# Attention stage: two moves of the softmax sums issued by SyncE one half pair later, the tanh ahead of the copy of the sums

## The reference

```python
xn = _layernorm(x, axis=-1)
# attention on xn
q = (x @ Wq.T + bq).reshape(B, S, N_HEADS, D_K)
...
scores = jnp.einsum('bqhd,bkhd->bhqk', q, k) * SCALE
mask = _local_mask(S)[None, None]          # (j <= i) & (j >= i - 128)
scores = jnp.where(mask, scores, jnp.float32(-10000.0))
attn = jax.nn.softmax(scores, axis=-1) + jnp.float32(1e-09)
ctx = jnp.einsum('bhqk,bkhd->bqhd', attn, v).reshape(B, S, D_MODEL)
return ctx @ Wo.T + bo
...
# feed forward on xn: 2 of 8 experts by gate, and one shared expert
h = jax.nn.silu(g) * u
eo = jnp.einsum('bem,emh->beh', h, down_proj_w)
combined = jnp.einsum('beh,be->bh', eo, c)
...
x = x + attention + combined + shared_out
```

## Time and profile before

| | |
|---|---|
| median of 3 runs | 1829.69 us (1823.14 to 1830.5) |
| profiled execution | 1809.16 us, its span 1807.4 us |
| TensorE busy | 1631.9 us (90%) |
| VectorE, ScalarE, GpSimd busy | 1157.8, 967.5, 1049.6 us (64%, 54%, 58%) |
| one masked maximum (L1526), mean | 385 ns |
| one copy of sums (L1431) | 0.60 us, 64 of them |

### The profile page before, as it was taken

The page is one execution under the profiler, slowest core; times in us unless marked ns, Lnnn a source line. Parts: engine busy times, 40 slices in busy tenths (PEclk is TensorE's granted clock), DMA queues, the critical chain, the costliest instruction groups (busy, mean ns, idle before and its releaser), DMA issues.

```text
span 1807.4 us, 38460 instructions
## 1 busy us (share of the span) xinstructions
PE 1631.9 (90%) x11441; PEld 1330.0 (74%) x11441; DVE 1157.8 (64%) x3852; ACT 967.5 (54%) x1914; POOL 1049.6 (58%) x1139
## 2 busy tenths in 40 slices
PE   5888874999999999999999789989898898889987
PEld 4666663888898888888888556666676666666665
DVE  5899973666666566666656656665666666666652
ACT  3545432545545454454544356666666666666663
POOL 0888886222122221212220269888898888888888
PEclk9989996999999999999999589999999999999999
DMA  4577646444444444444564466766666666667652
GB/s 132 199 246 246 234 188 221 156 142 155 144 153 148 147 156 145 151 150 151 149 142 105 107 144 155 160 165 157 149 154 149 147 156 153 153 160 161 155 127 80
DMA packets 224801, 284.26 MB, mean 157 GB/s; under 512 B 59369, under 2 KB 143978, under 8 KB 224746
## 3 DMA queue, kind: packets, MB, share of 16 engines
q1 hardware_dynamic: 163898, 199.17, 39.4%
q10 hardware_dynamic: 47216, 47.20, 8.7%
q0 software_dynamic: 13632, 37.24, 8.3%
HBM read 193.61 MB, written 79.95 MB: 151 GB/s over the span
## 4 chain that ended last, share of the span: by engine, by line
PE 72%; POOL 9%; ACT 5%; DVE 5%; issue 4%; ACTq 3%; DMA 1%; DVEq 0%; POOLq 0%; SPq 0%
PE psum L151 42%; PE psum L817 12%; PE psum L1303 6%; PE psum L1263 5%; POOL plain_arena L389 3%; PE psum L1286 2%; POOL plain_arena L388 2%; PE psum L898 2%; ACT plain_arena L1417 2%; ACTq L1436 1%; ACTq L1437 1%; ACT plain_arena L1431 1%; DVE plain_arena L1541 1%; DVE plain_arena L1526 1%; ACT plain_arena L1449 1%
## 5 line engine op out<-in xcount | busy, mean ns | idle before, releaser
L151 PE MATMUL psum<-split_arena 128*128 128x512 f32 (+2 forms) x4560 | 1010.2, 373 | 59.4 <-DVE plain_arena L1541 55.2
L151 PEld LDWEIGHTS psum<-split_arena 128*128 128x128 f32 x4560 | 783.5, 198 | 208.0 <-DVE plain_arena L1541 57.5
L1526 DVE CUSTOM_DVE_ANT_0 plain_arena<-psum,mask 128x256 f32<-128x256 f32 (+1 forms) x1024 | 338.1, 385 | 211.7 <-PE psum L1263 211.3
L881 POOL DMA_INDIRECT plain_arena<-xn_d,order x156 | 156.5, 1003 | 509.7 <-PE psum L898 466.1
L1417 ACT ACTIVATE plain_arena<-psum 128x512 f32<-128x512 f32 (+1 forms) x512 | 250.3, 541 | 239.5 <-PE psum L1286 220.1
L817 PE MATMUL psum<-split_arena 128*128 128x256 f32 x1872 | 233.8, 285 | 0.0
L817 PEld LDWEIGHTS psum<-split_arena 128*128 128x128 f32 x1872 | 226.9, 192 | 0.1
L944 ACT ACTIVATE plain_arena<-psum 128x512 f32<-128x512 f32 x156 | 93.3, 598 | 221.1 <-PE psum L151 220.9
L995 DVE TENSOR_TENSOR plain_arena<-psum,plain_arena 128x512 f32<-128x512 f32 x156 | 107.7, 690 | 115.8 <-ACT plain_arena L944 112.8
L1263 PE MATMUL psum<-split_arena 48*128 48x256 f32 (+1 forms) x1024 | 156.7, 351 | 12.1 <-POOL plain_arena L1249 6.8
L1185 POOL TENSOR_SCALAR_AFFINE_SELECT plain_arena<-plain_arena 128x1024 f32<-128x1024 f32 x128 | 140.4, 1097 | 35.5 <-ACT plain_arena L1417 34.9
(11 more groups left out here) (163 smaller groups left out, 1869.0 us busy)
## 6 DMA issues: line engine op xcount, KB each, us to landing
plain_arena<-in_gate_w SPq DMA_DIRECT2D x39, 512.0 KB, 3.3
plain_arena<-in_up_w SPq DMA_DIRECT2D x39, 512.0 KB
plain_arena<-in_down_w SPq DMA_DIRECT2D x39, 512.0 KB, 3.5
y_d<-plain_arena ACTq DMA_DIRECT2D x39, 512.0 KB, 2.9
plain_arena<-in_x SPq DMA_DIRECT2D x32, 512.0 KB, 4.8
q_d<-split_arena SPq DMA_DIRECT2D x32, 512.0 KB, 3.6
k_d<-split_arena SPq DMA_DIRECT2D x32, 512.0 KB, 4.7
split_arena<-q_d SPq DMA_DIRECT2D x128, 128.0 KB, 3.6
```

What stands on the lines that cost most here:

```text
L151: last = pe.matmul(out, lhs_t(p), rhs(q), start=(begins and c == 0 and k == 0), stop=(ends and c == len(chunks) - 1 and k == 2), skip_grou ...
L881: pool.indirect_dma_start(c_x[:, a, :], None, xn_d, bass.IndirectOffsetOnAxis(order[:, T * blk + a:T * blk + a + 1], 0)).then_inc(c_ldx, 16)
L1526: last = dve.tensor_tensor_reduce(b_junk[:, 2 * par + i % 2, 0:cols], psum[:, par, at:at + cols], mask[:, 2 * P - cols:2 * P], -1.0, 3e38, ...
```

## The change

The two moves leave ScalarE's `copy_sums` and become `move_sums` on SyncE, one half pair later, behind what SyncE issues in the half pair before. Every later step of this route comes one half pair later as well (lags 17, 18, 19, 21, 22 and 23 become 18, 19, 20, 22, 23 and 24). In ScalarE's half pair the tanh stands ahead of the copy of the sums. Nothing is computed otherwise.

```diff
--- before.py
+++ after.py
@@ -1093,7 +1093,7 @@
 
 
         LAG_TM, LAG_M, LAG_T, LAG_SEL, LAG_V, LAG_U = 5, 6, 8, 10, 14, 15
-        LAG_RC, LAG_RS, LAG_SP, LAG_N, LAG_CH, LAG_CL = 17, 18, 19, 21, 22, 23
+        LAG_RC, LAG_RS, LAG_SP, LAG_N, LAG_CH, LAG_CL = 18, 19, 20, 22, 23, 24
 
         def turns(eng, turn):
 
@@ -1142,6 +1142,14 @@
                 sp.dma_start(b_vd[:, s, :, :], v_d[ds(b, 1), :, :, g * 64:(g + 1) * 64].rearrange(
                     "o p a c -> p (o a) c")).then_inc(b_ldv[s], 16)
 
+            def move_sums(b, g):
+                c, at = g // 2, 32 * (g % 2)
+                hold(sp, b_ue, 4 * b + g + 1)
+                sp.dma_start(b_zc[at:at + 32, c, :], b_u[1:P:32, g % 2, :]).then_inc(b_zl[g % 2], 16)
+                if g % 2 == 0:
+                    hold_after(sp, b_clo, 2 * b + c - 1)
+                sp.dma_start(b_uc[2 * at:2 * at + 64, c, :], b_u[0:P:2, g % 2, :]).then_inc(b_ul[g % 2], 16)
+
             def store_reciprocal(b, c):
                 hold(sp, b_rc, 2 * b + c + 1)
                 sp.dma_start(rz_d[c, :, :].rearrange("h (k s) -> (h k) s", s=64), b_rz[0:64, c, :]).then_inc(b_rs, 16)
@@ -1159,6 +1167,9 @@
                     b, c = due_chunk(t, h, LAG_SP)
                     if b is not None:
                         spread_reciprocal(b, c)
+                    b, g = due_group(t, h, LAG_U + 1)
+                    if b is not None:
+                        move_sums(b, g)
                     if h in (3, 7) and valid(t):
                         load_qk(sp, t, (h + 5) // 4)
                     if h in (11, 15) and valid(t + 1):
@@ -1429,12 +1440,6 @@
                 after(act, b_zl[g % 2], 16 * (2 * b + g // 2))
                 after(act, b_ul[g % 2], 16 * (2 * b + g // 2))
                 act.copy(b_u[:, g % 2, :], psum[:, 4, :]).then_inc(b_ue, 1)
-                c, at = g // 2, 32 * (g % 2)
-                act.wait_ge(b_ue, 4 * b + g + 1)
-                if g % 2 == 0:
-                    after(act, b_clo, 2 * b + c - 1)
-                act.dma_start(b_zc[at:at + 32, c, :], b_u[1:P:32, g % 2, :]).then_inc(b_zl[g % 2], 16)
-                act.dma_start(b_uc[2 * at:2 * at + 64, c, :], b_u[0:P:2, g % 2, :]).then_inc(b_ul[g % 2], 16)
 
             def context_hi(b, c):
                 act.wait_ge(b_uz, 2 * b + c + 1)
@@ -1483,12 +1488,12 @@
                     b, g = due_group(t, h, 12)
                     if b is not None:
                         interleave_values(b, g)
+                    b, m = step_due(t, h, 9)
+                    if b is not None:
+                        silu(b, m)
                     b, g = due_group(t, h, LAG_U)
                     if b is not None:
                         copy_sums(b, g)
-                    b, m = step_due(t, h, 9)
-                    if b is not None:
-                        silu(b, m)
                     b, m = chunk_due(t, h)
                     if b is not None:
                         hidden_hi(b, m)
```

## The result

The changed kernel is slower: its median is 1837.17 us (1827.35 to 1841.96, 13 runs), that of the kernel before beside it 1826.36 us (1817.38 to 1830.5, 13 runs). The ratio is 1.0054 with an interval of 1.0038 to 1.007, 10.8 us more where 19 us less were forecast. 1837 lies outside the range of 1794 to 1833 as well. The profiled execution after took 1839.04 us, its span 1837.3.

The account below looks back on a forecast made before the run. TensorE and GpSimd were near their limit, with TensorE stalling at gates behind ScalarE's late tanh. Gains of 0.51 + 0.68 = 1.19 us a turn, times 16, gave 19 us: median 1829.69 to 1811 us, range 1794 to 1833.

Parts of the forecast that it names:

- Moves on SyncE: Moves and spread of the reciprocals, issued behind SyncE's loads, land in time: costed at nothing, spread's margin 1.6 us.
- rival (c): Spread landing past 6.2 us delays TensorE at half pair (13) one for one; 1855 us at 9 us; chance 0.10.
- the second sum: From transposed scores of half pair (15) to sums of values of (6): 20.51 us, before 21.19, gaining 0.68 us a turn.
- The first sum: ScalarE's work between TensorE's transposed scores of half pairs (11) and (13): 5.83 us, before 6.34, gaining 0.51 us a turn.
- rival (b): No change: new stalls bring 1.2 GHz stretches where TensorE sets the pace, 1.5 us each; 1830 to 1835 us; chance 0.18.
- The stalls at the gates: TensorE's 1.80 us stall at the gate of half pair (12), and that at (0), vanish with the tanh first.
- rival (a): Stalls just vanish and GpSimd bounds: 3.9 us a turn, 63 us, 1767 us; chance 0.10, partly filled included.

Follow-up runs that it names:

- the second profile: Kernel before and changed kernel each run once more, nothing edited, for another profile: 1823.02 us and 1841.34 us.

## Why the prediction was wrong

**The step that failed** is the one on the spread in "Moves on SyncE": "Margin 1.6 us, at 5.7 us still 0.5 us. So nothing either". The term that was mis-sized is the landing. It was taken as 4.6 to 5.7 us from the loads of v, half as large; GpSimd's waits end 5.4 to 8.2 us after the issue, median 6.5 over 14 turns, and 6.3 to 8.2, median 6.8, in the second profile. In part of the turns the issue came later too. The prediction let it start 5.8 us after the transposed scores of (7), from the trace of before, where the load of v began 5.0 us after these scores. In the turn shown the load of v began at 6.4 and the spread at 7.2 us, and in seven of 14 turns the spread goes out at 6.5 to 7.3; in the other seven, and in all but one turn of the second profile, it goes out by 5.8 us. The turn shown makes 7.2 + 7.0 + 1.3 = 15.5 us, where ScalarE was ready at 1364.23, the end of its L1458: 13.5 us after (7), which the prediction had as 13.28. The difference of 2.0 us is ScalarE's idleness there. The mechanism was rival (c), with its condition (landing over 6.2 us) and its one-for-one price right, and a chance of 0.10 far too low for a term that was called the least trusted. Over the 14 turns the normalising ends 13.0 to 15.9 us after (7), past 13.28 in 12 of them. ScalarE comes to the exponentials of (12) 1.0 us later in the mean than the 4.72 us after (11) of the prediction, and 16 x 1.0 is what the spread before the load of v gave back (0.9%, 16 us). That the late spread is the cause is shown from both sides: issued later, +2.7%; issued earlier in three ways, -0.9, -1.0 and -1.2%. Of the 30 us between forecast and result these are some 16; the rest, some 13, is what that kernel lacks of the forecast, 0.3% gained and not 1%, and belongs to the second sum and the clock.

**The first sum** (5.83 us from (11) to (13)) was right once the spread is in time: 5.84 us in the turn shown with the spread before the load of v, 5.83 in the mean. With the late spread it is 7.16, more than the 6.64 of before: +0.5 instead of -0.5 us. What the sum has at nothing is the row maxima. Their transfers land later than before, and TensorE's new wait for them at (12) is larger than that at (13). In the first profile it hides behind ScalarE's lateness; in the second the exponentials of (12) wait for TensorE in five of 14 turns, by 0.3 to 1.7 us. Why transfers of 8 KB land some 2 us later no run tests. With the spread issued before the load of v they come 1.3 us sooner than in the changed kernel, so part of what that run gained may be theirs. With the spread issued first of all, or by ScalarE, most of the wait at (12) is there, 13.3 and 13.9 us in 14 turns, and the gain is as large, so they are not its main part.

**The second sum** was right in kind and too large. ScalarE does wait for GpSimd at (5) (29.3 us in 14 places), TensorE at (5) and (6) behind it. But (15) to (6) takes 21.02 us in the mean (20.87 in the median, 20.94 in the turn that ends at 1347.48), and 20.8 to 20.9 where the spread is in time, not 20.51: instead of 0.68 us some 0.2 to 0.3 us are gained on 21.04 (21.16 in the median). In the turn that ends at 1347.48 the chain begins 2.98 us after the transposed scores of (15) instead of 2.73. GpSimd ran up to there without a pause, so it was not ScalarE, as assumed, that it came from.

**The clock**, rival (b), came as well. The forecast let the low clock of (0) fall into waits that cost nothing. It did leave (0), but to behind the stalls at (5) and (6), and at (12) to (14), where TensorE sets the pace: (6) to (7) takes 4.17 us in the mean instead of 3.27, (13) to (15) 6.66 instead of 6.21. The falls between (11) and (15) go mostly with the late spread: seven and eight of 13 turns have one in the two profiles of the changed kernel, none has with the spread before the load of v or issued by ScalarE, and three have with it issued first of all, behind the wait at (12). Those behind (5) and (6) stay. With the spread before the load of v eight of 13 turns take 4.6 to 5.1 us from (6) to (7) and 48.2 to 48.6 us in all, the other five 3.3 and 46.8 to 47.3, and this is a large part of why that kernel gains 0.3% and not the forecast 1%. That the stalls cause the falls at (5) and (6) is only argued from where they stand. The prediction held against this rival that the stall at (12) brought no fall in the turn that it read; in two other turns of the same trace it did, and they take 48.6 us. Its time for a fall in half of the turns is off as well: by its own price that is 1829.69 - 16 x (1.19 - 0.75) = 1823 us and not 1826.

**The stalls at the gates** vanished as forecast (0.5 us left of 49.9), and rival (a) was far off. **The moves** on SyncE were rightly costed at nothing, as far as their own landing goes: VectorE's reciprocals (L1559) wait 12.2 us in 12 places, in its idle time, and TensorE 1.6 us in all for VectorE's maxima and gate factors. With the spread issued by ScalarE, and the moves still by SyncE, the kernel stands at 0.9932 and the tanh alone at 0.9945, with intervals that overlap: beyond the tanh the moves bring nothing that can be measured either.

**Open.** The two pairs of profiles differ by 29.9 and 18.3 us (1839.04 to 1809.16, 1841.34 to 1823.02), the medians by 10.8. How much the low clock takes varies between executions of the same kernel, and no run here says by what. No run takes away the wait for the row maxima alone. So of the 10.8 us I can give the sign and the cause, and not an account to the microsecond.

## What to carry to other kernels

A transfer that is moved behind others in an issuing engine's list is late twice: by the time that its issuer needs for all that stands ahead (here 4.4 to 6.7 us for nine loads), and by a landing behind them. Its margin has to be reckoned with both at their worst, and where the margin is half a microsecond, the chance of loss is not small. Other transfers of the same time can land later too, even small ones of another list: look at every wait for a transfer there, also where the profile calls its releaser "issue". When a stall is taken away, look at the buffers' and totals' waits that the shifted steps now meet: one of them named an engine's later step where an earlier one was enough, and one changed semaphore with the spread issued elsewhere made the change that lost 0.5% one that gains 1.5%.

## What the runs showed of the hardware

One transfer of 256 KB took 4.7 to 6.9 us from its issue to the end of GpSimd's wait where it stood behind eight loads of q and k, and 5.4 to 8.2 us where the load of v stood ahead as well, in 14 turns each. Issuing is not steady either: in the turns shown SyncE took 4.0 us from its first load to the spread behind eight (1341.56 to 1345.55), and 6.6 us behind nine, with a pause of 1.5 us (1351.91 to 1353.41) in the middle of the loads. Five of 14 turns of this profile have such a pause and none of the second profile; the cause stays open.

Two transfers of 8 KB issued by ScalarE at (10) had landed by 3.9 us after the second issue in the median turn of the kernel before, where TensorE did not wait for them. In the changed kernel TensorE stood until 4.4 to 7.0 us after it, median 5.9, with SyncE's transfers around them moved and nothing of theirs changed but the time. What holds them up is not shown.

In the kernel before, turns with one stretch at 1.2 GHz take 47.6 to 47.7 us where it stands behind the stall at (0) and 48.6 where it stands behind that at (12), and turns with two take 49.1 to 49.2. One execution had a second stretch in none of 13 turns and another in seven. A single profile of such a kernel can therefore be a per cent off its median.
